# Attention maxima of two heads in one entry: row groups for the scores, one reduction, totals in two column groups, key copies on ScalarE

## The chip, the core and the metric

The kernel runs on one core of one Trainium2 chip. The metric is device time in microseconds, the median of a few executions. The profiled execution is one further run, whose trace the rows below come from. The engines are PE (TensorE matmul), PEld (TensorE weight load), DVE (VectorE), ACT (ScalarE), POOL (GpSimd) and SP, which issues most DMAs.

## What is computed

One transformer layer on x of shape (4, 2048, 256): attention with 4 heads of 64, rotary positions and a causal mask, then a layer norm, a routed feed-forward layer with 32 experts, and a second layer norm. The change touches the attention alone:

```
q, k = (_rope(q), _rope(k))
mask = jnp.where(jnp.tril(jnp.ones((T, T), dtype=bool)), 0.0, -jnp.inf).astype(x.dtype)
energy = jnp.einsum('bhtd,bhld->bhtl', q, k) + mask
attn = jax.nn.softmax(energy, axis=-1)
out = jnp.einsum('bhtl,bhld->bhtd', attn, v)
```

## The kernel before, in words

Attention works on 8 head pairs (4 batches of 2 pairs), each with 2048 tokens in 16 tiles of 128. A **group** y is one pair with 512 queries, G = 0 to 3; there are 32 groups. A **unit** u is one head of a group (64 of them). For a group the keys are walked in blocks of 128, the two heads in turn, so the whole program has 640 **chunks**. The program is written out as 670 **slots**, one chunk to a slot in the first 640, and every engine walks the same slots in the same order (function `walk`). What else runs in a slot (projections, transposes of queries and keys, totals, output projection, norm) is planned by `Plan` into lists `early` and `late`.

A chunk g goes through these steps. In slot g-2, PE multiplies keys by queries into `scores_t_ps` (L545 with the upper parts and the lower part of the keys, L546 with the lower part of the queries and a row of ones that adds the negative row maximum). ACT takes the exponential (L674). DVE or POOL adds the result to running sums (L370). Every fourth slot PE multiplies four chunks with the values (L562); there each head writes 64 of the 128 output columns of the array, so two heads use two column groups.

The maximum that L546 adds has to be known first. It comes from **entries**: for a block of 128 queries (i) and 512 keys (c), PE computes the scores the other way round (L526, and L529 adds the mask on the diagonal block c == G) into one of the two banks of `scores_ps`, and DVE reduces them to a maximum (L796, `part_max`). After the last entry of a unit DVE reduces the partial maxima (L801, `neg_pad`), a **row entry** transposes them on PE (L515, four transposes), and ACT copies the row into `q_low` (L683). Entry e may start when the bank of entry e-2 has been read. There are 640 entries (384 of full blocks, 256 on the diagonal) and 64 row entries. The planner sets an entry per slot, two at most where it has to catch up.

A key tile goes: PE transposes it (L471), ACT writes the upper part (L655, `k_st`), DVE the lower part (L766), and POOL copies the upper part into `k_one` (L907). A query tile: PE transposes, ACT writes the upper part twice (L701, `q_two`, partitions 0 to 63 and 64 to 127), DVE the lower part (L821, `q_low`). The totals of a group are 8 matmuls on PE with 8 output columns (L594), a reciprocal on DVE, and 4 matmuls that spread the result over 128 columns (L601, 8 rows).

Of the kernel before, what the change touches and what calls it, by code (L numbers as in the profile page):

```python
# [7 lines left out]
P = 128  # L8
HEADS = 4
HD = 64  # L10
D = 256
# [42 lines left out]
CH = 512  # L54
# [15 lines left out]
class Plan:  # L70

    def __init__(self, NB, NT):
# [91 lines left out]
        for y, (f, G) in enumerate(self.groups):  # L164
            at = min(s for s, u, _, _ in entries if u // 2 == y) - 10
# [13 lines left out]
        rows, at, placed, taken = [], -100, [], {}  # L179
        for wanted, u, c, i in entries:  # L180
            y = self.units[u][0]
            f = self.groups[y][0]
            s = max(wanted, at)
            if u >= 4:
                s = max(s, q_from[y])
            s = max(s, turned.get(f * NT + 4 * c + 3, -100) + 1)
            while s >= 0 and s < begin[y] - 6 and taken.get(s, 0) >= 2:
                s += 1
            taken[s] = taken.get(s, 0) + 1
            at = s  # L190
            while rows and (rows[0][0] <= s or rows[0][1] < 2 <= u):
                placed.append((min(rows[0][0], s), rows.pop(0)[1], None, None))
            placed.append((s, u, c, i))
            if (c, i) == (self.size[u] // 4 - 1, 3):
                assert s <= begin[y] - 3, (u, s, begin[y])
                rows.append((min(s + 2, begin[y] - 3), u))
        placed += [(s, u, None, None) for s, u in rows]
        self.score_at = [[] for _ in range(slots)]
        self.before, self.emptied = [], []
        for e, (s, u, c, i) in enumerate(placed):  # L200
            self.entries.append((u, c, i))
            if c is None:
                self.row_entry[u] = e
                assert s <= begin[u // 2] - 3 and len(self.row_entry) == u + 1
                self.emptied.append(("row", u + 1))
            else:
                self.last_entry[u] = e
                self.emptied.append(("score", e + 1 - len(self.row_entry)))
            (self.before if s < 0 else self.score_at[s]).append(e)
        assert all(self.row_entry[u - 2] < self.last_entry[u] for u in range(2, len(self.units)))  # L210
# [21 lines left out]
def attention(nc, dram, NB, NT):  # L232
# [43 lines left out]
    with ExitStack() as ctx:  # L276
# [12 lines left out]
        k_one = sb("k_one", [HD + 1, 2, KEEP * P], F32R)  # L289
# [4 lines left out]
        q_low = sb("q_low", [HD + 1, Q_RING, 2, CH], F32R)  # L294
        probs = sb("probs", [P, P_RING, CH])
        sums = sb("sums", [P, 2, 2, CH])
        pick = sb("pick", [P, 8, 8])
        spread = sb("spread", [P, 4, 2, HD])
        inverse = sb("inverse", [8, P])
        attn = sb("attn", [P, 2, NT * P])  # L300
        neg_pad = sb("neg_pad", [P, 2, 4, HD + 1])
        part_max = sb("part_max", [P, 4, 4, 4])
# [72 lines left out]
        def walk(main, step, score, ahead):  # L375
# [9 lines left out]
            early_units = [e for e in plan.before if plan.entries[e][0] < 2]  # L385
# [66 lines left out]
        def _(pe):  # L452
# [49 lines left out]

            keys_seen, ones_seen, values_seen = [0], [0], [0]

            def score(e):
                u, c, i = plan.entries[e]
                f, G, hh, ring = unit(u)
                out = x_ps[:, e % 2, :]
                if e >= 2:
                    kind, count = plan.emptied[e - 2]  # L510
                    pe.wait_ge(row_read if kind == "row" else score_read, count)
                if c is None:
                    pe.wait_ge(neg_ready, u + 1)
                    for t in range(4):
                        mm = pe.transpose(out[0:HD + 1, cols(t)], neg_pad[:, u % 2, t, :], ident[:])  # L515
# [6 lines left out]
                if latest >= keys_seen[0]:  # L522
                    keys_seen[0] = latest + 1
                    pe.wait_ge(k_lower, latest + 1)
# [1342 lines left out]
```

## Time and profile before

| | us |
|---|---|
| median of 3 runs | 2308.29 |
| lowest, highest | 2306.02, 2310.01 |
| profiled execution, device time | 2305.32 |
| its span, first to last instruction | 2303.5 |
| attention, with its start and end | 0 to 1470 of the span |
| routing | 1470 to 1690 |
| experts and the last norm | 1690 to 2303.5 |

Over the span PE is busy for 1910.4 us (83%), DVE for 1589.0 (69%), POOL for 1388.5 (60%), ACT for 1141.5 (50%). The last chain of the page lies wholly in the final norm and says nothing of the attention. A stage is read from the windows and from the waits inside it. A busy PE is not PE at its peak, since a matmul's record reaches to the modelled end of its pipeline and overlaps the next; what one matmul costs is read from the start of it to the start of the next.

### The profile page before, as it was taken

The page shows a single profiled execution, that of the slowest core. Times are in us where ns is not written, and L with a number is a line of the kernel's source. Part 1 is how long each engine was busy: PE and PEld are TensorE (multiplying, and loading weights), DVE is VectorE, ACT ScalarE, POOL GpSimd, SP SyncE. Part 2 cuts the span into 40 slices and gives each one's busy share as a digit, 9 for nine tenths or more (in the row PEclk, how much of TensorE's full clock was granted, in tenths as well). Part 3 has the DMA queues.
Part 4 walks back from the last instruction along what each step waited for, and adds up shares of the span by engine and source line. Part 5 has one row for each costly group of instructions (what it writes and reads, how often), then busy time and mean ns, then how long its engine had stood idle before and what let it go on. Part 6 is the DMA issues. An engine that isn't in the chain of part 4 may idle for free. (4 is left out here: it accounts for less than half of the span.)

```text
span 2303.5 us, 37026 instructions
## 1 busy us (share of the span) xinstructions
PE 1910.4 (83%) x10914; PEld 1421.0 (62%) x10914; DVE 1589.0 (69%) x3363; ACT 1141.5 (50%) x2709; POOL 1388.5 (60%) x1723
## 2 busy tenths in 40 slices
PE   5899998998998898998998998452277999999990
PEld 4555655655655555655655554351176999999980
DVE  8576776787777777787777775356794665566555
ACT  3344455455455444455444444224264666666655
POOL 3368777677777676777777644210075676667652
PEclk7799999999999999999999999555588999999995
DMA  2000011111011111011111011130003435554428
GB/s 76 7 12 17 22 40 33 38 42 33 21 35 35 38 38 37 17 40 33 42 35 38 8 42 49 36 140 1 0 1 122 137 129 160 164 153 139 148 53 292
DMA packets 100610, 144.06 MB, mean 63 GB/s; under 512 B 17956, under 2 KB 88592, under 8 KB 96364
## 3 DMA queue, kind: packets, MB, share of 16 engines
q1 hardware_dynamic: 84588, 132.04, 16.7%
q0 software_dynamic: 15872, 10.24, 2.7%
q8 instruction: 67, 1.10, 0.2%
q14 instruction: 83, 0.68, 0.1%
HBM read 113.14 MB, written 39.85 MB: 66 GB/s over the span
## 5 line engine op out<-in xcount | busy, mean ns | idle before, releaser
L674 ACT ACTIVATE probs<-scores_t_ps 128x512 f32<-128x512 f32 (+3 forms) x640 | 339.6, 533 | 495.7 <-PE scores_t_ps L546 295.7
L796 DVE TENSOR_REDUCE part_max<-scores_ps 128x1 f32<-128x512 f32 (+3 forms) x640 | 372.6, 599 | 87.8 <-PE scores_ps L526 52.9
L370 POOL TENSOR_TENSOR sums<-sums,probs 128x512 f32<-128x512 f32 (+3 forms) x288 | 328.2, 1139 | 19.0 <-ACT probs L674 13.4
L526 PE MATMUL scores_ps<-k_st,q_two 128*128 128x512 f32 (+3 forms) x640 | 273.7, 446 | 68.9 <-DVE q_low L821 31.3
L1571 PE MATMUL up_ps<-xe_t,w 128*128 128x320 f32 x1920 | 289.7, 311 | 1.7 <-DVE xe_t L1678 1.7
L562 PE MATMUL out_ps<-probs,v_sb 128*64 128x512 f32 (+3 forms) x1280 | 287.1, 568 | 0.2 <-ACT probs L674 0.2
L1571 PEld LDWEIGHTS up_ps<-xe_t,w 128*128 128x128 f32 x1920 | 284.9, 190 | 1.9 <-issue 1.9
L545 PE MATMUL scores_t_ps<-q_two,k_st 128*128 128x512 f32 (+3 forms) x640 | 274.1, 428 | 8.3 <-ACT probs L674 8.1
L370 DVE TENSOR_TENSOR sums<-sums,probs 128x512 f32<-128x512 f32 (+3 forms) x288 | 257.9, 896 | 2.2
L546 PE MATMUL scores_t_ps<-q_low,k_one 65*128 65x512 f32 (+3 forms) x640 | 239.5, 374 | 0.0
L1534 POOL DMA_INDIRECT acc_rows<-out_rows,token x96 | 148.7, 1549 | 127.5 <-ACT out_rows L1661 116.5
L526 PEld LDWEIGHTS scores_ps<-k_st,q_two 128*128 128x128 f32 x640 | 125.8, 201 | 133.4 <-DVE part_max L796 62.4
L1692 DVE SCALAR_TENSOR_TENSOR h<-silu,up_ps 128x320 f32<-128x320 f32 x160 | 77.1, 482 | 183.0 <-ACT silu L1648 183.0
L545 PEld LDWEIGHTS scores_t_ps<-q_two,k_st 128*128 128x128 f32 x640 | 125.6, 196 | 125.2 <-issue 110.7
L1571 PE MATMUL y_ps<-w,h_parts 128*128 128x256 f32 x1440 | 181.2, 285 | 0.0
L1571 PEld LDWEIGHTS y_ps<-w,h_parts 128*128 128x128 f32 x1440 | 174.7, 192 | 2.2
L1514 POOL DMA_INDIRECT rows<-x_rows,token_in x96 | 128.9, 1342 | 48.0 <-POOL token_in L1511 28.4
L562 PEld LDWEIGHTS out_ps<-probs,v_sb 128*64 128x64 f32 x1280 | 82.8, 143 | 121.1 <-issue 105.7
L1673 DVE TENSOR_TENSOR w<-w_raw,w 128x768 fp32r<-128x768 f32 x160 | 153.0, 958 | 5.0 <-ACT w L1626 1.2
L949 POOL TENSOR_TENSOR x<-powers_of,power 128x2 f32<-128x2 f32 x64 | 54.3, 849 | 151.9 <-DVE powers_of L867 151.9
L959 POOL TENSOR_TENSOR products<-qk,cos_sin 128x256 f32<-128x256 f32 x116 | 88.1, 760 | 92.4 <-ACT qk L646 69.9
L1626 ACT CAST w<-w_raw 128x768 fp32r<-128x768 f32 x160 | 131.7, 825 | 7.4 <-PEq L992 7.4
(317 smaller groups left out, 3941.4 us busy)
## 6 DMA issues: line engine op xcount, KB each, us to landing
w_raw<-in_w_expert SPq DMA_DIRECT2D x32, 1536.0 KB, 6.5
x_t<-in_x_t SPq DMA_DIRECT2D x128, 128.0 KB, 2.0
w_raw<-in_w_adapter SPq DMA_DIRECT2D x32, 384.0 KB, 7.2
x_row<-in_x SPq DMA_DIRECT2D x64, 128.0 KB, 2.0
x_rows<-x SPq DMA_DIRECT2D x64, 128.0 KB, 2.0
acc_rows<-x SPq DMA_DIRECT2D x64, 128.0 KB, 2.0
ln_x<-acc_rows SPq DMA_DIRECT2D x16, 512.0 KB, 6.1
out_rows_dram<-ln_y SPq DMA_DIRECT2D x16, 512.0 KB, 5.2
```

The source lines that it names most:

```text
L370: eng.tensor_tensor(side, side, probs[:, g % P_RING, i * P:CH], ALU.add).then_inc(summed[u % 2], 1)
L526: mm = pe.matmul(out[:, 0:n], q_two[:, ring, hh, cols(i)], k_st[:, hh, places(f * NT + 4 * c, 4)][:, 0:n], start=True, stop=not diagonal)
L545: pe.matmul(out, k_st[:, hh, places(f * NT + kb)], q_two[:, ring, hh, i * P:CH], start=True, stop=False)
L546: mm = pe.matmul(out, k_one[:, hh, places(f * NT + kb)], q_low[:, ring, hh, i * P:CH], start=False, stop=not diagonal)
L562: mm = pe.matmul(o_ps[hh * HD:(hh + 1) * HD, i * P:CH], v_sb[:, place(f * NT + kb), hh, :], probs[:, g % P_RING, i * P:CH], start=kb == 0, ...
L674: act.activation(probs[:, g % P_RING, i * P:CH], s_ps[:, g % 2, i * P:CH], ACT.Exp).then_inc(exp_done, 1)
L796: dve.tensor_reduce(part_max[:, u % 4, i, c:c + 1], x_ps[:, e % 2, 0:n], AX.X, ALU.max).then_inc(score_read, 1)
L1514: pool.indirect_dma_start(out=rows[0:n, r, t, :], out_offset=None, in_=dram["x1"], in_offset=bass.IndirectOffsetOnAxis(ap=token_in[0:n, r, ...
L1534: pool.indirect_dma_start(out=dram["acc"], out_offset=bass.IndirectOffsetOnAxis(ap=token[0:n, r, t:t + 1], axis=0), in_=out[0:n, r, t, :], ...
L1571: mm = pe.matmul(o, left(a), right(b), start=start and n == 0, stop=stop and n == 2)
L1626: act.copy(columns(w[:, r, 0], p), columns(w_raw[:, r], p)).then_inc(w_upper, 1)
L1673: dve.tensor_tensor(columns(w[:, r, 1], p), columns(w_raw[:, r], p), columns(raw(w[:, r, 0]), p), ALU.subtract).then_inc(w_split, 1)
```

## The change

Entries are now of a group, both heads in one: two matmuls of 64 rows, head 0 from partitions 0 to 63 and head 1 from 64 to 127, each into its own bank of `scores_ps`, from the upper parts of the keys alone; one DVE instruction reduces both banks. There are 320 entries and 32 row entries. As both banks belong to one entry, entry e waits for entry e-1. `k_one` and `q_low` of head 1 move to partitions 64 to 127, with row 0 as the row of ones and of the maximum, so that head 1's second score matmul has 128 rows where it had 65. The copies into `k_one` move from POOL to ACT, two for each key tile. The totals use two column groups of 32, the spread two groups of rows and columns. The planner's spacing changes from one slot to two.

```diff
-        for u in reversed(range(len(self.units))):
-            G = self.groups[self.units[u][0]][1]
+        for y in reversed(range(len(self.groups))):
+            G = self.groups[y][1]
...
-                    cur = min(cur - 1, begin[u // 2] - 6)
-                    entries.append([cur, u, c, i])
+                    cur = min(cur - 2, begin[y] - 7)
+                    entries.append([cur, y, c, i])
...
-            s = max(wanted, at)
+            s = max(wanted, at + 1 if at >= 0 else at)
...
-                out = x_ps[:, e % 2, :]
-                if e >= 2:
-                    kind, count = plan.emptied[e - 2]
+                if e >= 1:
+                    kind, count = plan.emptied[e - 1]
...
-                        mm = pe.transpose(out[0:HD + 1, cols(t)], neg_pad[:, u % 2, t, :], ident[:])
+                        pe.transpose(x_ps[0:HD + 1, 0, cols(t)], neg_pad[:, y % 2, t, 0:HD + 1], ident[:])
+                        mm = pe.transpose(x_ps[0:1, 1, cols(t)], neg_pad[:, y % 2, t, HD + 1:HD + 2], ident[:])
...
-                mm = pe.matmul(out[:, 0:n], q_two[:, ring, hh, cols(i)], k_st[:, hh, places(f * NT + 4 * c, 4)][:, 0:n],
-                               start=True, stop=not diagonal)
+                for hh in range(2):
+                    half = slice(hh * HD, (hh + 1) * HD)
+                    mm = pe.matmul(x_ps[:, hh, 0:n], q_two[half, ring, hh, cols(i)],
+                                   k_one[half, hh, places(f * NT + 4 * c, 4)][:, 0:n], start=True, stop=not diagonal)
...
-                        for i in range(4):
-                            n = 4 * hh + i
-                            mm = pe.matmul(out[0:8, 0:P], pick[:, n, :], sums[:, k % 2, hh, cols(i)],
-                                           start=n == 0, stop=n == 7)
+                    for i in range(4):
+                        for hh in range(2):
+                            mm = pe.matmul(out[32 * hh:32 * hh + 32, 0:P], pick[:, i, :], sums[:, k % 2, hh, cols(i)],
+                                           start=i == 0, stop=i == 3)
...
-                        mm = pe.matmul(out[:, cols(i)], spread[0:8, i].rearrange("p a b -> p (a b)"), inverse[:],
-                                       start=True, stop=True)
+                        for hh in range(2):
+                            row = slice(32 * hh, 32 * hh + 4)
+                            mm = pe.matmul(out[hh * HD:(hh + 1) * HD, cols(i)], spread[row, i, :], inverse[row, :],
+                                           start=True, stop=True)
...
+                act.wait_ge(k_upper, n + 1)
+                act.copy(k_one[0:HD, 0, places(n)], k_st[0:HD, 0, places(n)])
+                act.copy(k_one[HD:P, 1, places(n)], k_st[0:HD, 1, places(n)]).then_inc(k_again, 1)
...
-                    act.copy(q_low[HD:HD + 1, ring, hh, :], x_ps[HD:HD + 1, e % 2, :]).then_inc(row_read, 1)
+                    act.copy(q_low[HD:HD + 1, ring, 0, :], x_ps[HD:HD + 1, 0, :])
+                    act.copy(q_low[0:1, ring, 1, :], x_ps[0:1, 1, :]).then_inc(row_read, 1)
...
-            dve.memset(raw(k_one[HD:HD + 1, :, 0:FIRST * P]), 1.0)
+            dve.memset(raw(k_one[HD:HD + 1, 0, 0:FIRST * P]), 1.0)
+            dve.memset(raw(k_one[0:HD, 1, 0:FIRST * P]), 0.0)
+            dve.drain()
+            dve.memset(raw(k_one[0:1, 1, 0:FIRST * P]), 1.0)
...
-                dve.tensor_reduce(part_max[:, u % 4, i, c:c + 1], x_ps[:, e % 2, 0:n], AX.X, ALU.max).then_inc(score_read, 1)
+                dve.tensor_reduce(part_max[:, y % 2, :, i, c], x_ps[:, :, 0:n], AX.X, ALU.max).then_inc(score_read, 1)
...
-            def again_k(n):
-                pool.wait_ge(k_upper, n + 1)
-                pool.tensor_copy(k_one[0:HD, :, places(n)], k_st[0:HD, :, places(n)])\
-                    .then_inc(k_again, 1)
```

The order of instructions changes at these places. On PE, around a row entry near the middle of the attention, before (the row entry is `ident,neg_pad`, an entry is `k_st,q_two`, the brackets are the semaphores waited for):

```order
L515 MATMUL scores_ps<-ident,neg_pad 65x128 [waits neg_ready,score_read]
L515 MATMUL scores_ps<-ident,neg_pad 65x128 x3
L526 MATMUL scores_ps<-k_st,q_two 128x512 [waits score_read]
L526 MATMUL scores_ps<-k_st,q_two 128x512 [waits row_read]
L562 MATMUL out_ps<-probs,v_sb 64x512 [waits exp_done] x4
L545 MATMUL scores_t_ps<-q_two,k_st 128x512 [waits exp_done]
```

Behind the row entry an entry of the other bank follows at once; only the one after that waits for ACT to have read the row.

The same engine around a row entry of the change (the last of its eight transposes, then the next entry with its two heads and two masks):

```order
L514 MATMUL scores_ps<-ident,neg_pad 65x128
L515 MATMUL scores_ps<-ident,neg_pad 1x128
L528 MATMUL scores_ps<-k_one,q_two 128x128 [waits k_again,q_split,row_read]
L528 MATMUL scores_ps<-k_one,q_two 128x128
L532 MATMUL scores_ps<-causal,ident_b 128x128 x2
L567 MATMUL out_ps<-probs,v_sb 64x512 [waits v_copied,exp_done]
```

The entry right behind the row entry now waits for `row_read` itself, and the value matmuls stand behind it. In the planned order an entry stands in the row entry's own slot for 9 of the 32 groups. Of the other steps from one entry to the next, 194 are two slots and 120 are one slot long.

On ACT, in slot 297, where the last query tile of a group and a key tile are turned together, before:

```order
L720 ACTIVATE x<-y,x_shift,rstd 128x256 [waits x1_turned,x1_stored1,shift_ready]
L674 ACTIVATE probs<-scores_t_ps 128x512 [waits summed0,values_done,scores_ready]
L655 CAST k_st<-misc_c_ps 128x2x128 [waits scores_ready,kt_turned]
L701 CAST q_two<-misc_b_ps 128x2x128 [waits qt_turned]
L674 ACTIVATE probs<-scores_t_ps 128x512 [waits summed1,values_done,scores_ready]
```

And of the change, in the same slot:

```order
L684 ACTIVATE probs<-scores_t_ps 128x512 [waits summed0,values_done,scores_ready]
L662 CAST k_st<-misc_c_ps 128x2x128 [waits scores_ready,kt_turned]
L664 COPY k_one<-k_st 64x128 [waits k_upper]
L665 COPY k_one<-k_st 64x128
L712 CAST q_two<-misc_b_ps 128x2x128 [waits qt_turned]
L684 ACTIVATE probs<-scores_t_ps 128x512 [waits summed1,values_done,scores_ready]
```

The two key copies stand between the key cast and the query cast, and the first waits for the key cast to have ended.

## Rows read from the trace of the kernel before

**Rows 1.** Windows by stage: us; busy us (instructions) of PE, PEld, DVE, ACT, POOL; clock

```profile
100.00:750.00 650.00, 596.93 (x3194) 382.11 (x3194) 479.07 (x1000) 316.98 (x834) 478.21 (x659) 0.97 0.10 29
750.00:1400.00 650.00, 590.80 (x3174) 380.10 (x3174) 484.49 (x1092) 315.02 (x845) 441.25 (x607) 0.96 0.11 34
1690.00:2250.00 560.00, 534.51 (x3788) 518.27 (x3786) 342.49 (x584) 352.52 (x686) 372.67 (x318) 0.98 0.40 124
```

**Rows 2.** Waits, 100 to 1400 us: who for whom, us, times, longest

```profile
PE scores_ps L526 <- DVE q_low L821: 29.3, 13, 3.3
...
PE scores_ps L526 <- DVE part_max L796: 21.0, 47, 1.9
...
PE scores_ps L526 <- ACT q_low L683: 9.4, 21, 0.7
```

**Rows 3.** Groups by shape, 100 to 1440 us: busy us, mean ns | idle before

```profile
L796 DVE TENSOR_REDUCE part_max<-scores_ps 128x1 f32<-128x512 f32 x428 | 283.2, 678 | 52.8 <-PE scores_ps L526 48.4 <-PE scores_ps L529 0.6 <-issue 0.2
...
L526 PE MATMUL scores_ps<-k_st,q_two 128*128 128x512 f32 x428 | 197.2, 477 | 52.1 <-DVE q_low L821 29.3 <-DVE part_max L796 13.5 <-ACT q_low L683 5.4
...
L907 POOL CAST k_one<-k_st 64x256 fp32r<-64x256 f32 x115 | 57.3, 499 | 42.4 <-ACT k_st L655 42.4
...
L713 ACT CAST attn_t<-attn 128x256 fp32r<-128x256 f32 x60 | 24.5, 409 | 0.0
...
L796 DVE TENSOR_REDUCE part_max<-scores_ps 128x1 f32<-128x128 f32 x59 | 16.6, 282 | 7.5 <-PE scores_ps L529 6.8 <-issue 0.2
```

**Rows 4.** Timeline of PE, pieces from 692 to 707 us: start, us

```profile
692.20 1.91 PE L594 MATMUL misc_c_ps<-sums,pick 128*8 128x128 f32 x16
...
694.38 0.23 PE L529 MATMUL scores_ps<-causal,ident_b 128*128 128x128 bf16 x1
694.42 0.48 PE L545 MATMUL scores_t_ps<-q_two,k_st 128*128 128x512 f32 x1
...
698.55 0.40 PE L546 MATMUL scores_t_ps<-q_low,k_one 65*128 65x512 f32 x1
698.88 0.37 PE L601 MATMUL misc_c_ps<-inverse,spread 8*128 8x128 f32 x1
...
698.88 1.15 PE L601 MATMUL misc_c_ps<-inverse,spread 8*128 8x128 f32 x8
699.96 0.32 PE L515 MATMUL scores_ps<-ident,neg_pad 128*65 128x128 f32 x1
...
701.38 0.40 PE L546 MATMUL scores_t_ps<-q_low,k_one 65*128 65x512 f32 x1
701.62 0.38 PE L617 MATMUL misc_c_ps<-ident,x 128*128 128x128 f32 x2
...
704.72 1.94 PE L562 MATMUL out_ps<-probs,v_sb 128*64 128x512 f32 x8
706.59 0.50 PE L545 MATMUL scores_t_ps<-q_two,k_st 128*128 128x512 f32 x1
706.93 0.40 PE L546 MATMUL scores_t_ps<-q_low,k_one 65*128 65x512 f32 x1
```

**Rows 5.** Timeline of ACT, PE and DVE, around 700 and 709 to 715 us

```profile
700.65 0.58 ACT L683 CAST q_low<-scores_ps 1x512 fp32r<-1x512 f32 x1 [0.78 <-PE scores_ps L515]
...
709.59 0.60 ACT L720 ACTIVATE x<-y,x_shift,rstd 128x256 f32<-128x256 f32 x1 [1.34 <-POOL x_shift L944]
...
711.99 0.83 PE L526 MATMUL scores_ps<-k_st,q_two 128*128 128x512 f32 x2 [3.25 <-DVE q_low L821]
...
714.16 1.27 DVE L796 TENSOR_REDUCE part_max<-scores_ps 128x1 f32<-128x512 f32 x2
```

**Rows 6.** Timeline of DVE and PE in the first 50 us

```profile
2.19 2.62 DVE L752 MEMSET k_one<- 1x3072 f32 x1 [0.68 <-issue]
...
46.52 2.62 DVE L781 MEMSET k_one<- 1x3072 f32 x1 [0.58 <-issue]
...
49.19 0.69 PE L471 MATMUL misc_a_ps<-ident,q_rows 128*128 128x128 f32 x2 [4.13 <-DVE k_one L781]
```

More of the change, by code:

```diff
@@ L164, in __init__ @@
         for y, (f, G) in enumerate(self.groups):
-            at = min(s for s, u, _, _ in entries if u // 2 == y) - 10
+            at = min(s for s, g, _, _ in entries if g == y) - 10
             if y >= Q_RING:
@@ L178, in __init__ @@
         self.entries, self.last_entry, self.row_entry = [], {}, {}
[L179 to L182, printed above, removed]
-            s = max(wanted, at)
-            if u >= 4:
+        rows, at, placed = [], -100, []
+        for wanted, y, c, i in entries:
+            f, G = self.groups[y]
+            s = max(wanted, at + 1 if at >= 0 else at)
+            if y >= 2:
                 s = max(s, q_from[y])
@@ L186, in __init__ @@
             s = max(s, turned.get(f * NT + 4 * c + 3, -100) + 1)
-            while s >= 0 and s < begin[y] - 6 and taken.get(s, 0) >= 2:
-                s += 1
-            taken[s] = taken.get(s, 0) + 1
             at = s
-            while rows and (rows[0][0] <= s or rows[0][1] < 2 <= u):
+            while rows and (rows[0][0] <= s or rows[0][1] < 1 <= y):
                 placed.append((min(rows[0][0], s), rows.pop(0)[1], None, None))
[L193 to L196, printed above, removed]
@@ L197, in __init__ @@
-        placed += [(s, u, None, None) for s, u in rows]
+            placed.append((s, y, c, i))
+            if (c, i) == (G, 3):
+                assert s <= begin[y] - 4, (y, s, begin[y])
+                rows.append((min(s + 2, begin[y] - 3), y))
+        placed += [(s, y, None, None) for s, y in rows]
         self.score_at = [[] for _ in range(slots)]
         self.before, self.emptied = [], []
-        for e, (s, u, c, i) in enumerate(placed):
-            self.entries.append((u, c, i))
+        for e, (s, y, c, i) in enumerate(placed):
+            self.entries.append((y, c, i))
@@ L202, in __init__ @@
             if c is None:
-                self.row_entry[u] = e
-                assert s <= begin[u // 2] - 3 and len(self.row_entry) == u + 1
-                self.emptied.append(("row", u + 1))
+                self.row_entry[y] = e
+                assert s <= begin[y] - 3 and len(self.row_entry) == y + 1
+                self.emptied.append(("row", y + 1))
             else:
-                self.last_entry[u] = e
+                self.last_entry[y] = e
                 self.emptied.append(("score", e + 1 - len(self.row_entry)))
@@ L209, in __init__ @@
             (self.before if s < 0 else self.score_at[s]).append(e)
-        assert all(self.row_entry[u - 2] < self.last_entry[u] for u in range(2, len(self.units)))
+        assert all(self.row_entry[y - 2] < self.last_entry[y] for y in range(2, len(self.groups)))
         for m, (at, turn, last) in enumerate(post):
@@ L384, in walk @@
             turned(0, 4)
-            early_units = [e for e in plan.before if plan.entries[e][0] < 2]
+            early_units = [e for e in plan.before if plan.entries[e][0] < 1]
             for e in early_units:
@@ L545, in ahead @@
                 pe.matmul(out, k_st[:, hh, places(f * NT + kb)], q_two[:, ring, hh, i * P:CH], start=True, stop=False)
-                mm = pe.matmul(out, k_one[:, hh, places(f * NT + kb)], q_low[:, ring, hh, i * P:CH], start=False, stop=not diagonal)
+                rows = one_rows(hh)
+                mm = pe.matmul(out, k_one[rows, hh, places(f * NT + kb)], q_low[rows, ring, hh, i * P:CH],
+                               start=False, stop=not diagonal)
                 if diagonal:
@@ L780, in _ @@
                 lower_k(x_ps[:, n % 2, 0:D], n)
-            dve.memset(raw(k_one[HD:HD + 1, :, FIRST * P:KEEP * P]), 1.0).then_inc(ones_set, 1)
+            dve.memset(raw(k_one[0:HD, 1, FIRST * P:KEEP * P]), 0.0)
+            dve.drain()
+            dve.memset(raw(k_one[0:1, 1, FIRST * P:KEEP * P]), 1.0)
+            dve.memset(raw(k_one[HD:HD + 1, 0, FIRST * P:KEEP * P]), 1.0).then_inc(ones_set, 1)
             split(w_o, w_raw[:, W_O:W_R1])
@@ L789, in score @@
             def score(e):
-                u, c, i = plan.entries[e]
-                f, G, hh, ring = unit(u)
+                y, c, i = plan.entries[e]
+                G = groups[y][1]
                 if c is None:
@@ L913, in _ @@
                 lower_xt(n)
-                if n >= 4:
-                    again_k(n - 4)
-            for n in range(FIRST - 2, FIRST):
-                again_k(n)
             def nothing(g):
```

75 lines of the change are left out of this document (40 added, 35 removed).

## The prediction

> **What bounds the kernel now.** I read the windows first, because the last chain of the page lies in the final norm and the change lies in the attention. From 100 to 1400 us PE is busy for 92% and 91% of the two halves, DVE for 74%, POOL for 74% and 68%, ACT for 49% [rows 1]. The reader is to see that PE is the engine nearest to its limit there, and that it runs at a granted clock of 0.97, so mostly at 2.4 GHz. From 1690 us on PE is fuller still, in work that the diff doesn't touch.
>
> Second come the waits in that stretch, of which I need those of PE alone. They are short: 29.3 us in 13 pieces for the lower part of a query tile, 21.0 us in 47 pieces for DVE's reading of a score bank, 9.4 us for ACT's reading of the maximum row [rows 2]. So an instruction taken from PE is worth most of its time, and one that PE has to wait for is worth a part of it. Third I read PE instruction by instruction, since the price of a matmul is the distance to the start of the next one.
>
> **Totals and spread.** The totals are 16 records (8 fp32 matmuls, two records each) in 1.91 us, about 0.11 us each [rows 4]. Do two column groups run side by side? The value matmuls show it: 8 records of 512 columns, two heads in two column groups, take 1.94 us [rows 4]. One record of 512 columns at the rate of the totals would be 4 x 0.11 = 0.44 us, so eight in a line would be 3.5 us; they run as four pairs. The totals then become 8 pairs, 0.87 us less in each group, 32 x 0.87 = 28 us. The spread goes from 8 records (1.15 us together [rows 4]) to 16 in 8 pairs: nothing if they pair, 32 x 0.9 = 28 us more if they don't. I take nothing, since its pairs lie in different column groups too.
>
> **Scores on PE.** Before, a matmul of 512 columns costs 0.24 us if its weights were loaded beside the one ahead (L546 at 701.38, next at 701.62) and 0.34 us if not (L545 at 706.59, next at 706.93); its own record is then 0.50 us against 0.40 [rows 4]. The mean of 477 ns for L526 with 512 columns [rows 3] says that about three in four are of the dear kind, so one costs about 0.32 us and the two heads 0.63 us.
>
> What 64-row matmuls cost among 128-row ones is nowhere in the trace. The nearest rows are the spread's 8-row matmuls. Into them: L546 at 698.55, next at 698.88, 0.33 us in place of 0.24; and the first takes 0.37 us, where the other seven add (1.15 - 0.37) / 7 = 0.11 us each and a record is about 0.27 us long, 0.10 us more. Out of them: the last starts at about 698.88 + 1.15 - 0.27 = 699.76, the next matmul at 699.96, 0.20 in place of 0.11; and the first matmul behind a change of this kind is 0.10 us longer (L545 at 706.59, behind the 64-column value matmuls) [rows 4]. A round trip is thus 0.09 + 0.10 + 0.09 + 0.10 = 0.38 us. The Trainium skill ("TensorEngine Tiling (Array Packing)", Key Properties) says that changing the tiling mode drains TensorE, while changing only the tile doesn't; by that rule each pair pays the trip, as the rows of 8-row matmuls do, and without the rule PE would save some 100 us more below. No row here shows 64 rows.
>
> If the two row groups overlap as the column groups do, a full-block pair costs 0.24 + 0.38 = 0.62 us. Where it stands right ahead of the value matmuls (115 of 308 entries in the planned order) the way out is one that is paid there already, and it costs 0.43 us. Mean 0.55 against 0.63: 192 x 0.08 = 15 us gained. On the diagonal, with 320 columns in the mean, a head cost 0.15 + 0.08 + 0.04 for the mask (L529 at 694.38, next at 694.42 [rows 4]), two heads 0.54; the pair costs 0.19 + 0.15 + 0.14 to leave, and two masks of 0.05, 0.58: 128 x 0.04 = 5 us lost. Together **10 us gained**, so the pairing is nearly eaten by the changes of mode. Bounds: no overlap costs 192 x 0.24 + 128 x 0.15 = 65 us more; weight loads that don't overlap 320 x 0.1 = 32 us more; no price for the mode 100 us less (192 x 0.31 + 128 x 0.33).
>
> PE's work falls by 28 + 10 = 38 us. I let three quarters of it reach the time, **28 us**, because other engines are at three quarters themselves [rows 1].
>
> **DVE.** A reduction of 512 columns takes 678 ns, of 128 columns 282 ns [rows 3], so 1.03 ns a column and 0.15 us fixed; 1024 columns take 1.21 us in place of 2 x 0.68. That is 0.15 us for 320 entries, 48 us of DVE time. Entry e now waits for e-1, but it holds both banks, and the step to the next is two slots mostly; a slot is about 2.2 us (640 chunks in the 1400 us of the attention). I take **10 us** of the 21.0 us wait [rows 2] as gained.
>
> **Row entries.** ACT's row copy is 0.58 us and starts 0.04 us after the transposes [rows 5]. An entry right behind the row entry used to have the other bank. Now, in the 9 groups where it shares the slot, PE stands for two copies and a little, 1.3 us, with the value matmuls and the next scores queued behind: 12 us lost. The old wait of 9.4 us [rows 2] goes. Net **3 us lost**.
>
> **Key copies.** They leave POOL, 57.3 us [rows 3], and come to ACT: an SBUF copy of 256 columns takes 409 ns there [rows 3], so one of 128 about 0.3, two some 0.5 us behind one another with the wait for the cast ahead. ACT is idle half the time and hides 115 of them. The cover is gone where a query tile turns in the same slot: its cast comes 0.5 us later, DVE's lower part too, and PE waits for that already (3.25 us at 711.99 [rows 5]). 13 such waits x 0.5 = **6 us lost**.
>
> **Start.** Each memset of 3072 elements takes 2.62 us [rows 6] and becomes 4608 elements in three: 1.3 us more each. PE stood 4.13 us for the second one [rows 6], and the first holds up the weights, less 0.35 us that DVE waits anyway for their load. With the 12 entries ahead of slot 0 no longer alternating between banks, some 2 us: **4 us lost**.
>
> **Relief.** The 48 us of DVE and 57 us of POOL shorten queues that ACT and PE wait behind, as ACT does 1.34 us for a shift from POOL at 709.59 [rows 5]. I take **5 us gained**, bounds 0 and 40.
>
> **Sum.** -28 - 10 + 3 + 6 + 4 - 5 = -30 us. The profiled execution took 2305.3 us, its span 2303.5; that makes 2275. The median of the runs lies 3 us above the profiled one: **2278 us**.
>
> **Rivals.**
> - *The single pair of banks stalls PE* (slower). The two matmuls at 711.99 are read by DVE from 714.16 to 715.43 [rows 5], 3.4 us after they start, longer than the 2.2 us of a slot. 120 entries come one slot after another, and behind a waiting one stand the value matmuls and the next scores of PE's queue. At 0.7 us each this is 84 us, 2350 at worst; half of them at that, 2320. From a mean of 0.25 us (30 us) it decides the sign. Against it: before, entries in twos had the same distance to their bank, and that cost 21.0 us in all.
> - *The row groups don't overlap.* 65 us of PE and 28 us of the spread, three quarters of it: 2278 + 70 = about 2348; weights alone in line, 2302. For it: no row with two row groups. Against: the column pairs.
> - *The change doesn't do what it says for the time*: PE's shorter work turns into longer waits for DVE and ACT, since they set the pace of a slot by latency. What is left is the start and the rows: 2300 to 2310. Against: PE's 92%.
> - *More comes back*: a free change of mode (2278 - 0.75 x 100 = 2203) or POOL and DVE relieved in full (2243). For it: ACT and PE wait mostly behind short chains over these two. Against: the 8-row rows.
>
> **Chances.** The forecast, 2255 to 2300: 0.48. More comes back, 2200 to 2255: 0.16. No time effect: 0.10. Stall at the banks: 0.15. No overlap: 0.11. The range from 2238 to 2328 leaves out the tail of the better case and the ends of the two worse ones. 0.2% is 4.6 us, about what a measurement of this kernel can tell from no change: faster gets the forecast, the better case and a little of the third, 0.66; same 0.10; slower 0.24.
>
> **What would show it.** Right: the two score matmuls of an entry start within some 10 ns, with 0.1 us of drain on either side; totals in half of 1.91 us; the DVE reduction near 1.21 us, 320 of them; PE waiting about 1.3 us for the row copies at 9 places; PE's longest waits still for the lower query part, 0.5 us longer. Wrong: waits of PE for `part_max` above 50 us in all, score matmuls 0.2 us apart, a spread of 1.9 us, or a lower granted clock in the attention.

## The result, and the profile after

The changed kernel takes 2366.66 us (median of 4 runs, 2360.38 to 2372.56) against 2307.15 us for the kernel before on the same chip (2298.63 to 2310.01): the ratio is 1.0261, 95% interval 1.0236 to 1.0286. It is 60 us slower where 29 us less were forecast, and lies above the range. The profiled execution took 2372.56 us, its span is 2370.7 us.

The windows of the attention come first (columns as in [rows 1]).

```profile
100.00:750.00 650.00, 572.56 (x3194) 342.57 (x3194) 435.27 (x788) 337.30 (x919) 434.99 (x572) 0.93 0.09 28
750.00:1400.00 650.00, 570.27 (x3146) 345.35 (x3144) 439.53 (x854) 331.50 (x916) 416.48 (x551) 0.92 0.10 31
```

Each engine but ACT does less in the same 650 us than in [rows 1], and PE's granted clock is down from 0.97 and 0.96 to 0.93 and 0.92. With two levels, 1.2 and 2.4 GHz, a mean of 0.965 means that 7% of the 1300 us passed at 1.2 GHz, 91 us, and 0.925 that 15% did, 195 us. Work that falls into such time lasts twice as long, so the 104 us more cost up to 52 us. PE's waits in the same stretch, as in [rows 2]:

```profile
PE scores_ps L528 <- DVE part_max L813: 50.0, 70, 2.4
PE scores_ps L528 <- DVE q_low L838: 36.3, 16, 3.8
PE scores_ps L528 <- ACT q_low L694: 16.3, 9, 2.1
...
PE scores_ps L514 <- DVE neg_pad L818: 12.6, 15, 1.6
```

The first three were 59.7 us together in [rows 2] and are 102.6 us now. The wait of the row transposes for `neg_pad` is 12.6 us, where the same view of before has this:

```profile
PE scores_ps L515 <- DVE neg_pad L801: 2.9, 7, 0.6
```

Waits and clock together (43 + 10 + up to 52) are about 100 us, what is left of the loss when the 38 us of PE work that the prediction took away are put back. The whole of the attention, from the first exponential to the end of the last, shows it more plainly (columns as in [rows 1]; before, then after):

```profile
63.80:1445.40 1381.60, 1257.66 (x6654) 803.45 (x6654) 1011.26 (x2213) 665.39 (x1768) 955.64 (x1309) 0.95 0.10 32
68.10:1512.20 1444.10, 1258.76 (x6902) 752.28 (x6901) 963.67 (x1866) 730.53 (x2000) 908.50 (x1193) 0.92 0.10 30
```

It is 62.5 us longer. PE idles in it for 185 us in place of 124, 61 us more, and is busy as long as before, though the change takes work away; the lower clock is the likely reason. Idle time and a lower clock rise together in most of the kernels below, so they need not be two separate causes; that the one brings the other was not tested by itself.

The work itself became cheaper as forecast. Groups by shape, 100 to 1400 us, against [rows 3]:

```profile
L813 DVE TENSOR_REDUCE part_max<-scores_ps 128x2 f32<-128x1024 f32 x210 | 256.4, 1221 | 70.2 <-PE scores_ps L528 55.3 <-PE scores_ps L532 10.6
...
L664 ACT CAST k_one<-k_st 64x128 fp32r<-64x128 f32 x116 | 34.6, 298 | 3.7
L665 ACT CAST k_one<-k_st 64x128 fp32r<-64x128 f32 x116 | 34.4, 297 | 1.4
```

One read of both heads is 1.22 us (forecast 1.21), a key copy 0.30 (forecast 0.3). The timeline of PE (start, us), to be held against [rows 4, 5]:

```profile
726.81 0.39 PE L550 MATMUL scores_t_ps<-q_low,k_one 65*128 65x512 f32 x1
727.13 0.50 PE L528 MATMUL scores_ps<-k_one,q_two 64*128 64x512 f32 x2
727.56 0.29 PE L532 MATMUL scores_ps<-causal,ident_b 128*128 128x128 bf16 x2
727.65 0.48 PE L548 MATMUL scores_t_ps<-q_two,k_st 128*128 128x512 f32 x1
727.97 0.40 PE L550 MATMUL scores_t_ps<-q_low,k_one 128*128 128x512 f32 x1
728.29 1.07 PE L599 MATMUL misc_c_ps<-sums,pick 128*32 128x128 f32 x16
729.29 0.50 PE L548 MATMUL scores_t_ps<-q_two,k_st 128*128 128x512 f32 x1
...
734.62 1.09 PE L608 MATMUL misc_c_ps<-inverse,spread 4*64 4x128 f32 x16
```

Both score matmuls of 512 columns end within 0.50 us, the length of a single one; two of 128 rows took 0.83 us in [rows 5]. So the row groups run side by side. From the matmul ahead to the pair pass 0.32 us, where 0.24 us pass in [rows 4], and 0.43 us from the pair to the next start. The totals take 1.07 us in place of 1.91, the spread 1.09 in place of 1.15. What the change loses is seen at a row entry, in the timeline of DVE, PE and ACT:

```profile
709.82 1.22 DVE L813 TENSOR_REDUCE part_max<-scores_ps 128x2 f32<-128x1024 f32 x1
...
711.13 0.19 DVE L818 TENSOR_REDUCE neg_pad<-part_max 128x8 f32<-128x32 f32 x1
...
711.47 0.30 PE L514 MATMUL scores_ps<-ident,neg_pad 128*65 128x128 f32 x1 [1.00 <-DVE neg_pad L818]
...
713.40 0.58 ACT L693 CAST q_low<-scores_ps 1x512 fp32r<-1x512 f32 x1
...
713.99 0.57 ACT L694 CAST q_low<-scores_ps 1x512 fp32r<-1x512 f32 x1
...
714.61 0.48 PE L528 MATMUL scores_ps<-k_one,q_two 64*128 64x128 f32 x2 [2.09 <-ACT q_low L694]
```

From the last read (709.82) to the next scores (714.61) pass 4.8 us, more than two slots of 2.2 us. PE waits first for the maximum and then, its transposes done at 712.5, until both copies of the row have left the only pair of banks; ACT starts them 0.9 us late. An entry in the other bank could have been made meanwhile.

### The profile page after: what moved, and what is told of

It is laid out like the page before. It is cut to its first block and busy times, and to the rows that moved or that the text cites. A ratio compares the mean times of both kernels' runs of the same rounds, so it can differ in the third digit from the quotient of the medians.

```text
span 2370.7 us, 37201 instructions
## 1 busy us (share of the span) xinstructions
PE 1908.3 (80%) x11170; PEld 1366.0 (58%) x11170; DVE 1542.1 (65%) x3015; ACT 1213.8 (51%) x2965; POOL 1336.8 (56%) x1597
## 3 DMA queue, kind: packets, MB, share of 16 engines
q1 hardware_dynamic: 84588, 132.04, 16.3%
## 5 line engine op out<-in xcount | busy, mean ns | idle before, releaser
L813 DVE TENSOR_REDUCE part_max<-scores_ps 128x2 f32<-128x1024 f32 (+2 forms) x320 | 338.8, 1059 | 116.4 <-PE scores_ps L528 59.0
L548 PE MATMUL scores_t_ps<-q_two,k_st 128*128 128x512 f32 (+3 forms) x640 | 296.7, 464 | 10.0 <-ACT probs L684 8.6
L567 PE MATMUL out_ps<-probs,v_sb 128*64 128x512 f32 (+3 forms) x1280 | 302.1, 596 | 0.2 <-ACT probs L684 0.2
L528 PE MATMUL scores_ps<-k_one,q_two 64*128 64x512 f32 (+3 forms) x640 | 163.6, 507 | 118.4 <-DVE part_max L813 63.0
L366 DVE TENSOR_TENSOR sums<-sums,probs 128x512 f32<-128x512 f32 (+3 forms) x288 | 240.4, 835 | 3.3 <-ACT probs L684 0.3
L550 PE MATMUL scores_t_ps<-q_low,k_one 65*128 65x512 f32 (+7 forms) x640 | 241.9, 378 | 0.0
L968 POOL TENSOR_TENSOR products<-qk,cos_sin 128x256 f32<-128x256 f32 x116 | 93.4, 805 | 212.6 <-ACT qk L653 212.5
L528 PEld LDWEIGHTS scores_ps<-k_one,q_two 64*128 64x128 f32 x640 | 65.5, 200 | 198.9 <-DVE part_max L813 94.7
L453 PE MATMUL misc_a_ps<-w_qkv,x_t_parts 128*128 128x384 f32 x576 | 143.9, 392 | 1.0 <-DVE q_low L838 0.7
L958 POOL TENSOR_TENSOR x<-powers_of,power 128x2 f32<-128x2 f32 x64 | 49.4, 771 | 162.0 <-DVE powers_of L883 162.0
```

The costliest lines, as they stand in the source:

```text
L366: eng.tensor_tensor(side, side, probs[:, g % P_RING, i * P:CH], ALU.add).then_inc(summed[u % 2], 1)
L453: mm = pe.matmul(out, parts_l(a), parts_r(b), start=start and n == 0, stop=stop and n == 2)
L528: mm = pe.matmul(x_ps[:, hh, 0:n], q_two[half, ring, hh, cols(i)], k_one[half, hh, places(f * NT + 4 * c, 4)][:, 0:n], start=True, stop=no ...
L548: pe.matmul(out, k_st[:, hh, places(f * NT + kb)], q_two[:, ring, hh, i * P:CH], start=True, stop=False)
L550: mm = pe.matmul(out, k_one[rows, hh, places(f * NT + kb)], q_low[rows, ring, hh, i * P:CH], start=False, stop=not diagonal)
L567: mm = pe.matmul(o_ps[hh * HD:(hh + 1) * HD, i * P:CH], v_sb[:, place(f * NT + kb), hh, :], probs[:, g % P_RING, i * P:CH], start=kb == 0, ...
```

## Experiments

Theory 1: the single pair of banks makes TensorE wait for VectorE's reads, and the clock falls in these waits. Theory 2: the key copies make ScalarE late. Theory 3: the row groups by themselves pull the granted clock down. Theory 4, added later: it is the long read for both heads, not the depth of the banks. Each ratio is to the kernel before, in runs on the same chip.

**Full-row scores in the changed kernel.**

```diff
-mm = pe.matmul(x_ps[:, hh, 0:n], q_two[half, ring, hh, cols(i)], k_one[half, hh, places(...)]...
+mm = pe.matmul(x_ps[:, hh, 0:n], q_two[:, ring, hh, cols(i)], k_st[:, hh, places(...)]...
```

> The changed kernel with each head's score matmul over all 128 rows again (both parts of the keys), the heads one after the other; the single pair of banks, the one read for both heads, ScalarE's key copies and the totals in column groups stay. Theory 1 (the single pair of banks: a score waits until VectorE has read the one before, and the clock falls in those waits): the waits stay and each pair is up to 0.1 us longer on TensorE, so 2365 to 2395 us, with about 50 us of waits for part_max and a granted clock of 0.92 to 0.93 between 100 and 1400 us, as in the changed kernel. Theory 3 (the row groups themselves pull the granted clock down): the clock comes back to 0.96 or more and the time to 2305 to 2335 us.

2369.13 us, ratio 1.0296 [1.0274, 1.0317]: the loss stays, with 59.3 us of waits for `part_max` and a clock of 0.94 and 0.93. The row groups aren't its cause. They gain 0.3%, some 8 us, and the intervals overlap. The trace shows why it is so little. Two full-row matmuls of 512 columns take 0.53 us from the first to the next start behind them (mean of 112 without waits at 2.4 GHz), the second starting 0.24 us after the first; the pair in row groups takes 0.43 us (mean of 106) and 0.09 us more from the matmul ahead.

**Totals alone, in the kernel before.** The edit is the part of the change's diff on `pick`, `spread`, `inverse`, the `sum` and the `spread` step.

> The kernel before with only the totals and their spreading in column groups. The prediction's own term: 28 us less (2275 to 2290 us), since PE's share of the totals falls by half. Rival: the totals wait for the sums or the saved time turns into waits, 2298 to 2310 us.

2283.03 us, ratio 0.9931 [0.9903, 0.9958]: 16 us gained, 19 by the two medians (27 of PE work; of the forecast's 28 the sum let three quarters, 21 us, through).

**Key copies alone, in the kernel before.**

```diff
+act.wait_ge(k_upper, n + 1)
+act.copy(k_one[0:HD, 0, places(n)], k_st[0:HD, 0, places(n)])
+act.copy(k_one[0:HD, 1, places(n)], k_st[0:HD, 1, places(n)]).then_inc(k_again, 1)
...
-pool.tensor_copy(k_one[0:HD, :, places(n)], k_st[0:HD, :, places(n)])
```

> The kernel before with only the copies of the keys moved from GpSimd to ScalarE, two instructions for a tile (one for each head). Theory 2 (ScalarE's chains get late by the copies, and this is most of the loss): 2330 to 2365 us. Theory 1 or 3: the prediction's term of 6 us, with 3 more for the second copy at the start, so 2300 to 2322 us, with TensorE's waits for q_low of ScalarE under 16 us.

2279.11 us, ratio 0.9899 [0.9879, 0.9920]: 23 us faster, outside every expectation. Theory 2 falls. VectorE's addition of the exponentials, which copies no key, became cheaper. Its group by line, 100 to 1400 us, before the move and after it:

```profile
L370 DVE TENSOR_TENSOR sums<-sums,probs 128x512 f32<-128x512 f32 (+3 forms) x271 | 245.1, 905 | 2.0
```

```profile
L370 DVE TENSOR_TENSOR sums<-sums,probs 128x512 f32<-128x512 f32 (+3 forms) x277 | 212.2, 766 | 2.0
```

**The same with GpSimd's copies kept, into a buffer that nobody reads.**

```diff
+pool.wait_ge(k_upper, n + 1)
...
+pool.tensor_copy(k_spare[:, :, cols(n % 2)], k_st[0:HD, :, places(n)]).then_inc(spared, 1)
```

> The kernel before with the key copies by ScalarE (2279 us), while GpSimd goes on making its copies into a buffer that nobody reads. If the gain came because GpSimd's copies no longer hold up VectorE's additions: the mean addition on VectorE rises from 766 ns to 870 ns or more and the time to 2293 to 2312 us. If it came because the keys are ready earlier: 2274 to 2287 us.

```profile
L371 DVE TENSOR_TENSOR sums<-sums,probs 128x512 f32<-128x512 f32 (+3 forms) x271 | 242.6, 895 | 2.0
```

2307.07 us, ratio 1.0027 [1.0011, 1.0043]: the whole gain is gone, and the additions are at 895 ns again. So the gain is not that keys are ready earlier, but that GpSimd no longer makes the copies. The Trainium skill ("SBUF — State Buffer", Who interferes with whom) says that a VectorE instruction with two SBUF inputs contends with a GpSimd instruction that reads SBUF; an addition of two SBUF tiles is one. The trace of the kernel before agrees, in its timeline of POOL and DVE, a key copy first and a GpSimd addition second:

```profile
402.71 1.19 POOL L907 CAST k_one<-k_st 64x256 fp32r<-64x256 f32 x1
402.97 0.67 DVE L370 TENSOR_TENSOR sums<-sums,probs 128x512 f32<-128x512 f32 x1
...
1063.59 1.27 POOL L370 TENSOR_TENSOR sums<-sums,probs 128x512 f32<-128x512 f32 x1
1063.61 1.81 DVE L370 TENSOR_TENSOR sums<-sums,probs 128x512 f32<-128x512 f32 x1
```

Beside the copy alone the addition keeps its 0.67 us, and the copy takes 1.19 us where the shortest takes 0.39. So do all six additions of 512 columns that meet nothing but a copy. Beside GpSimd's own addition it takes 1.81 us. How the copies raise the mean of VectorE's additions is therefore open: they also take 57 us of GpSimd's queue and shift what it does next, and this run puts all of that back at once. The way from there to the time is not in TensorE's idle time either. With the copies on ScalarE, the attention reads:

```profile
62.60:1420.00 1357.40, 1237.43 (x6654) 794.16 (x6654) 967.49 (x2213) 715.04 (x2000) 916.62 (x1193) 0.97 0.10 32
```

TensorE idles for 120 us where it idled for 124; the same 6654 matmuls take it 20 us less, at a clock of 0.97 in place of 0.95.

**Half the columns read.** VectorE reads `x_ps[:, :, 0:n // 2]`; half of the maxima are left out.

> The changed kernel in which VectorE reads only the first half of each entry's columns (half of the maxima are left out), so a pair of banks is free after about 0.6 us instead of 1.06. Theory 1: the waits for part_max fall from 50 us to under 20, the granted clock between 100 and 1400 us rises to 0.95 or more, and the time falls to 2240 to 2310 us. Theories 2 and 3: the clock stays at 0.92 to 0.93 and the time at 2335 to 2370 us.

```profile
100.00:750.00 650.00, 591.51 (x3321) 353.14 (x3320) 385.32 (x830) 352.31 (x960) 462.78 (x600) 0.94 0.10 30
750.00:1400.00 650.00, 584.41 (x3334) 351.66 (x3335) 399.45 (x949) 349.17 (x965) 427.48 (x559) 0.94 0.11 35
```

2288.68 us, ratio 0.9940 [0.9919, 0.9961]: against the changed kernel the time falls by 3.1%, and the waits for `part_max` fall to 18.5 us. That is theory 1's case, but VectorE also has less to do here, so the run doesn't tell the wait from the length of the read (theory 4). The clock rises to 0.94 only.

**The same with full-row scores.** Both edits together.

> The half-read kernel (2289 us; half of the maxima are left out) with full-row scores in place of the row groups. If the row groups pay as soon as TensorE no longer waits for the reads (the prediction's term of 28 us): 2305 to 2325 us. Theory 3, that what the row groups save is given back in the granted clock: 2280 to 2296 us, with the clock between 100 and 1400 us up from 0.94 to 0.95 or more.

```profile
100.00:750.00 650.00, 581.66 (x3368) 375.14 (x3369) 393.07 (x848) 357.69 (x980) 470.49 (x609) 0.97 0.10 30
750.00:1400.00 650.00, 580.35 (x3354) 370.59 (x3352) 400.37 (x956) 350.66 (x967) 428.16 (x560) 0.95 0.11 35
```

2288.40 us, ratio 0.9945 [0.9925, 0.9965]: the same time with and without row groups. Without them PE's clock is 0.97 and 0.95, with them 0.94 and 0.94. So the row groups are no cause of the loss here either. Whether they lower the clock, as theory 3 says, is not settled: of the run without them the profile shows the execution with the highest clock of eight (0.893 over the whole kernel, mean of all 0.890), of the run with them the one with the lowest of four (0.885, mean 0.887).

**Totals and key copies together.** The two edits above on the kernel before.

> The kernel before with the two parts of the change that gained by themselves: totals in column groups (19 us less) and the copies of the keys by ScalarE (23 us less). If they save in different places the gains add: 2255 to 2268 us. If both only fill the same waits, 2270 to 2282 us. With theory 1 the first would mean that all the rest of the change, the pairs in one pair of banks, costs about 100 us.

2271.43 us, ratio 0.9870 [0.9842, 0.9899], 30 us gained, less than 16 + 23. The rest of the change thus costs some 90 us.

**One bank at a time.** On that kernel, `emptied[e - 2]` becomes `emptied[e - 1]` for every entry (one head).

> The same, but each score entry (one head, one bank, a read of about 0.56 us) waits until the entry before it has been read, so that the two banks are never both in use. Theory 1, that the loss is TensorE waiting because nothing can be made ahead of the read: 50 to 130 us more than without the wait (2310 to 2395 us), the waits for part_max over 50 us, and the granted clock between 100 and 1400 us down to 0.92 to 0.95. Theory 4, that the long read of both heads keeps VectorE from its other work and the depth doesn't matter: under 25 us more (2260 to 2290 us).

```profile
PE scores_ps L526 <- DVE part_max L801: 186.3, 203, 3.1
```

2708.35 us, ratio 1.1764 [1.1724, 1.1804], with a clock of 0.85 and 0.82: far above both expectations. A score that may not be made ahead of the read before it is dear: 437 us for 640 entries.

**Two slots again.** In the changed kernel with full-row scores an entry is made in two steps, each in one bank with both heads; the two widest diagonal entries of a group still take both banks.

```diff
+for lo, hi in ((0, (i + 1) * P),) if diagonal else ((0, 256), (256, 512)):
...
+    parts.append(((turn,), lo, hi, [last[turn]], made))
+    last[turn] = ("score", read)
+    turn = 1 - turn
```

> The changed kernel with full-row scores (2369 us) in which an entry of 512 keys is made in two steps of 256 keys for both heads, each step in one bank, so that one step can be made while VectorE reads the other; only the two widest diagonal entries of a group still take both banks at once. VectorE has as many reads as before the change, of 512 columns each. Theory 1: the waits for part_max fall under 25 us, the clock rises to 0.95 or more, and the time falls to 2255 to 2300 us. If the order of the entries or the pairing of the heads is the cause: 2335 to 2370 us.

2330.62 us, ratio 1.0134 [1.0103, 1.0165]: 1.6% less than with full-row scores and one pair of banks, about half of the least that theory 1 expected. The waits for `part_max` fall to 24.6 us, but those of the row entries stay (16.9 us for ACT, 12.9 us for `neg_pad`), since these still take both banks.

**Scores last in the slot, changed kernel.** `score(e)` moves behind `multiply` and `ahead` on PE, behind `exp` on ACT, behind `add_up` on DVE.

> The changed kernel with the scores behind the multiplications and the next exponentials' scores in each slot on TensorE, the row copies behind the exponentials on ScalarE, and the maxima behind the addition on VectorE. Theory 1: VectorE gets up to 1.5 us more before TensorE asks for the banks, so the waits for part_max fall to under 30 us, and the time to 2290 to 2345 us. Rival: the rows and maxima come a slot later, the wait only changes its place, and the time stays at 2350 to 2385 us.

2335.08 us, ratio 1.0145 [1.0113, 1.0178]. The time falls by 1.1% as theory 1 expected, but not for its reason: the waits for `part_max` are 55.7 us, more than before. Those for the lower query part fall from 36.3 to 10.9 us and for `neg_pad` from 12.6 us to nothing. It says little on the banks.

**Later row entries, changed kernel.** `rows.append((begin[y] - 3, y))` in place of `min(s + 2, begin[y] - 3)`.

> The changed kernel with each row entry moved from two slots behind the last score to the last slot allowed, three ahead of the group's first exponential, so the transposes no longer ask for the maxima at once. Theory 1 with the row term missized: TensorE's waits for neg_pad (12.6 us) go, and 10 to 30 us with them: 2335 to 2358 us. Rival: the row then holds the banks when the next scores want them, or the first exponentials wait for it: 2360 to 2385 us.

```profile
PE scores_ps L528 <- DVE part_max L813: 42.5, 55, 2.9
PE scores_ps L528 <- DVE q_low L838: 40.6, 16, 4.3
PE scores_ps L528 <- ACT q_low L694: 40.1, 28, 1.9
```

2382.48 us, ratio 1.0348 [1.0313, 1.0382], a miss and the rival's case: the scores behind the row now ask for the banks at once, 28 times in place of 9, and wait 40.1 us for ACT's copies.

**Order of the change, banks of before.** On the kernel with totals and copies the entries stand block by block with both heads behind each other, each head in its own bank and slot.

```diff
+for u in (2 * y + 1, 2 * y):
+    cur = min(cur - 1, begin[y] - 6)
+    entries.append([cur, u, c, i])
```

> The kernel before with totals in column groups and key copies by ScalarE (2271 us), and with the scores in the order of the change (block by block, both heads of a pair behind each other, both row entries at the end), but each head still in its own bank and read by itself, an entry waiting for the one before the last. If the order of the entries and the late, doubled row entry carry a good part of what two slots did not give back (60 us): 2295 to 2335 us. If depth and the reads of two banks are all: 2265 to 2285 us.

```profile
61.10:1413.10 1352.00, 1225.13 (x6903) 780.80 (x6902) 988.53 (x2213) 712.79 (x2000) 913.68 (x1193) 0.96 0.11 32
```

2268.75 us, ratio 0.9861 [0.9828, 0.9895]: the order costs nothing. The line shows the whole attention.

**Both heads in one slot.** On that, `cur = min(cur - 2 * (u % 2), begin[y] - 7)`. From slot 0 on every pair then stands in the slot that it has in the changed kernel.

> The same without the added wait: both heads of a pair in one slot, each entry waiting for the one before the last. It is the base for the two others. Theory 1: 2262 to 2285 us. If two scores in one slot are themselves the cost: 2295 us or more.

```profile
61.40:1446.90 1385.50, 1246.08 (x6902) 793.37 (x6901) 978.12 (x2213) 707.60 (x2000) 917.06 (x1193) 0.94 0.10 31
```

2305.57 us, ratio 1.0017 [1.0003, 1.0032]: 36 us for the placement alone, the second case of the expectation, which none of the theories held. The waits for `part_max` are even shorter (23.3 us against 37.9), but those of the row entries are longer (8.6 against 2.5 us for `neg_pad`, 10.5 against 1.3 for ACT). Over the attention TensorE idles for 139 us in place of 127 and takes 21 us more for the same matmuls, with the clock at 0.94 in place of 0.96.

**The added wait, for scores alone and for all.**

```diff
+if e >= 2 and hh == 0:
+    kind, count = plan.emptied[e - 1]
+    pe.wait_ge(row_read if kind == "row" else score_read, count)
```

> The kernel with totals in column groups, key copies by ScalarE and the order of the change (2269 us), both heads of a pair now in the same slot, each head in its own bank, made by full-row matmuls and read by itself, with one wait added: the first head of a pair waits until the second head of the pair before has been read (row entries too). This is the wait of the changed kernel alone, without its row groups and its one read for both heads. Theory 1: it carries most of the loss, 2325 to 2375 us, with over 45 us of waits for part_max. Theory 4 (the long read, the row entry's form and the start carry it): 2272 to 2300 us.

> The same with the added wait only between two score pairs, not before or behind row entries. If the row entries carry a good part of the wait's price: 15 to 40 us less than with all waits. If the reads of the maxima carry it: within 10 us of it.

```profile
PE scores_ps L530 <- DVE part_max L805: 54.7, 78, 2.3
...
PE scores_ps L530 <- ACT q_low L692: 14.1, 9, 2.0
PE scores_ps L519 <- DVE part_max L805: 12.8, 13, 1.6
```

For scores alone (the condition then leaves out pairs before and behind a row entry) 2335.47 us, ratio 1.0141 [1.0096, 1.0186]; for all 2351.14 us, ratio 1.0207 [1.0158, 1.0255], whose waits are shown. With separate reads and full-row matmuls the placement and the wait make nearly the changed kernel's picture of waits, and its clock (0.93 and 0.93). So the long read isn't needed for the loss, and theory 4 falls as its main cause (it expected 2272 to 2300 us). With the wait for scores alone the attention reads:

```profile
62.60:1479.10 1416.50, 1246.86 (x6902) 798.98 (x6901) 979.71 (x2213) 707.28 (x2000) 913.11 (x1193) 0.93 0.10 31
```

This wait is idle time: 170 us of it in place of 139, at the same busy time. Between the two waits the intervals overlap, so the share of the row entries is not firm.

**Scores last, with totals and copies.** The same move of `score(e)` on the kernel before with totals and copies.

> The kernel before with totals in column groups, key copies by ScalarE, and the scores behind the multiplications and the next exponentials' scores in each slot, as in the changed kernel with the scores last, where it gave 31 us. There are 24 us of waits for part_max and 37 us for q_low of VectorE to win here: 2245 to 2266 us if half of them go. If the wait only moves to the exponentials' scores, 2268 to 2280 us.

2265.14 us, ratio 0.9850 [0.9814, 0.9885]: 6 us less than without it, with overlapping intervals. It is the fastest version that ran, 1.5% faster than the kernel before and 4.0% faster than the change. Most of the expected gain moved: waits for the lower query part fall from 36.7 to 8.9 us, those of the exponentials' scores for ACT rise from 8.0 to 21.4 us.

## Why the prediction was wrong

The steps from the kernel before to the changed one, each ratio taken at 2302 us, the median of before beside the later runs:

| step | ratio | us |
|---|---|---|
| totals, key copies, order of the entries | 0.9861 | -32 |
| both heads of a pair in one slot | 1.0017 | +36 |
| the pair waits for the pair before (scores) | 1.0141 | +29 |
| the same at row entries | 1.0207 | +15 |
| one read for both heads, joint row entry, row groups, start | 1.0261 | +12 |

The last two steps are smaller than what the intervals of their ratios leave open; the first three are clear.

- **The failed step** is "I take 10 us of the 21.0 us wait [rows 2] as gained". The prediction saw that entry e now waits for e-1 and holds both banks, and took two slots for time enough. Measured, the wait costs 29 + 15 us, and what the two slots themselves need, both heads in one slot, 36 us more. This was the first rival, set at 0.7 us an entry, at worst 2350 us, and given a chance of 0.15. The wait's 44 us are about half of the 84 us of the rival's worst case; the placement, of which neither the sum nor the rival speaks, costs nearly as much again.
- The argument against that rival was that entries in twos had the same distance to their bank and cost 21.0 us in all. With all entries in twos the wait for `part_max` is indeed only 23.3 us; asking for the second head's read, which ends about 0.68 us later [rows 3], makes it 54.7 us with the waits at the row entries, 56.5 us without.
- **Clock.** No term of the sum held the granted clock, though the last sentence of the prediction named it. Of the 36 us of the placement 12 are idle time of TensorE and 21 are longer work at a lower clock: by the clock's records the attention has 156 us at 1.2 GHz in place of 112, which is up to 22 us lost. Why PE is granted less there isn't settled.
- **Totals and spread** were right: side by side, 0.84 us less in each of 32 groups or 27 us of PE work (28 forecast), 16 us of the time against 21 forecast.
- **Scores on PE** were right in mechanism: side by side, and nearly eaten up. Three quarters of 10 us were forecast; 8 us were measured in the one pair of kernels, with overlapping intervals, and none in the other. The Trainium skill ("TensorEngine Tiling (Array Packing)", Key Properties) says that a change of tiling mode drains TensorE. The trace agrees, with 0.08 us more ahead of the pair and 0.19 us more behind it than the 0.24 us between 128-row matmuls. The 0.63 us that the prediction took for two heads holds in the kernel before (0.31 us each, mean of 292); put behind each other with full rows they take 0.53 us, so that the row groups themselves had next to nothing to gain.
- **Row entries** had the right places (9 waits for ACT) at 16.3 us, 1.8 us each against 1.3 forecast. The term of 3 us was mis-sized: the same wait costs 15 us, as far as the overlapping intervals tell, because the transposes wait for the maximum too, and the last row's reading, seen above, holds the next scores.
- **Key copies and relief** had the wrong sign together: +6 and -5 forecast, 23 us gained. The bound of 40 us on the relief held the value; what was missed is what copies on GpSimd cost the rest. VectorE's mean addition and TensorE's clock move with them; by what chain is open.
- **Start**: the first exponential of the attention begins 4 us later than before (68.1 against 63.8 us), as forecast.
- **Still open** are the 12 us of the last line of the table, which weren't split, and across which the intervals of the two ratios overlap.

## What to carry to other kernels

Two buffers that are filled and read as one are one buffer: price such a merging by the wait of the next fill for the last read, in the slot order as planned, before counting the cheaper read, and price apart what it costs that two fills must then stand together. Where TensorE is over 90% busy, read the granted clock of the stretch beside every wait, since here it fell along with the new idle time. And test small moves by themselves: 57 us of copies moved off GpSimd were the best part of this change, where the sum had +6 and -5 us for them.

## What the runs showed of the hardware that was not expected

- Two matmuls of 64 rows in two row groups run side by side (0.50 us for two records of 512 columns), but among 128-row matmuls the pair took 0.52 us with its way in, against 0.53 for two of 128 rows, and the time was the same within 8 us.
- With 57 us of copies moved from GpSimd to ScalarE the kernel took 23 us less, VectorE's additions 766 ns in place of 905 in the mean, and TensorE 20 us less for the same matmuls. An addition of 512 columns took 0.67 us beside a lone GpSimd copy, whose time rose from 0.39 to 1.19 us, and 1.81 us beside a GpSimd addition.
- In these three kernels the granted clock fell as TensorE's idle time rose: over the attention 0.95 with 124 us of it, 0.92 with 185, and in the kernel with one bank at a time 0.85 and 0.82, with TensorE busy for 523 and 529 of each 650 us.
